# Another hand-written order of the steps, their lags and their PSUM banks, in a two-block kernel on one core

## The reference, cut to what matters

```
x = x + attn(layernorm(x))      # gated delta rule, 16 heads of 64
x = x + ffn(layernorm(x))       # softmax attention, then a mixture of 8 experts, 2 chosen
```

## Time and profile before

| | us |
|---|---|
| median of 3 runs | 5533.0 (5532.9 to 5550.23) |
| the profiled execution | 5533.59 |
| its span | 5531.7 |
| PE / DVE / ACT / POOL busy | 4792.2 / 4623.1 / 3445.0 / 2085.5 |

### The profile page before, as it was taken

The page is one execution under the profiler, slowest core; times in us unless marked ns, Lnnn a source line. Parts: engine busy times, 40 slices in busy tenths (PEclk is TensorE's granted clock), DMA queues, the critical chain, the costliest instruction groups (busy, mean ns, idle before and its releaser), DMA issues.

```text
span 5531.7 us, 111231 instructions
## 1 busy us (share of the span) xinstructions
PE 4792.2 (87%) x40448; PEld 3609.5 (65%) x40448; DVE 4623.1 (84%) x11457; ACT 3445.0 (62%) x6166; POOL 2085.5 (38%) x1485
## 2 busy tenths in 40 slices
PE   4688889988889898889898899888899888899986
PEld 2466667666667666667666677666677666677665
DVE  6888898888888888988888988888988888988852
ACT  3456666656666656766666666566666666666653
POOL 3443333443343442343443344433434433334420
PEclk7778898888888888988888888878988888888878
DMA  1001111011111011111111111111111011111011
GB/s 59 10 11 34 43 43 34 28 32 37 43 43 34 24 32 41 43 33 32 33 33 42 43 33 32 32 34 43 43 34 32 32 34 43 43 34 32 31 34 56
DMA packets 214453, 197.13 MB, mean 36 GB/s; under 512 B 13848, under 2 KB 176416, under 8 KB 209696
## 3 DMA queue, kind: packets, MB, share of 16 engines
q1 hardware_dynamic: 213920, 190.01, 11.1%
...
## 4 chain that ended last, share of the span: by engine, by line
DVE 52%; PE 38%; issue 8%; ACT 1%; SPq 0%; DMA 0%; POOL 0%; DVEq 0%; POOLq 0%; ACTq 0%
PE bank L984 36%; DVE acc L1390 10%; DVE tmpb L1556 6%; DVE NP L1526 6%; DVE Gam L1559 5%; DVE mx L1653 3%; DVE Gam L1512 3%; DVE moe L1738 2%; PE bank L988 2%; DVE QK L1671 1%; DVE QK L1479 1%; DVE Gam L1563 1%; DVE rot L1475 1%; DVE ms L1603 1%; DVE Kt L1543 1%
## 5 line engine op out<-in xcount | busy, mean ns | idle before, releaser
L1390 DVE SCALAR_TENSOR_TENSOR acc<-bank,conv_w,acc 128x255 f32<-128x255 f32 (+2 forms) x2304 | 925.1, 470 | 27.3 <-ACT acc L791 26.4
L717 POOL TENSOR_TENSOR sq<-acc 128x256 f32<-128x256 f32 x256 | 191.2, 747 | 1734.5 <-ACT acc L797 1722.3
L984 PE MATMUL bank<-QK 64*128 64x256 f32 (+1 forms) x4096 | 603.3, 352 | 211.8 <-DVE mx L1653 97.7
L984 PE MATMUL bank<-W,h 128*128 128x128 f32 x4096 | 579.7, 302 | 190.1 <-issue 103.3
L984 PEld LDWEIGHTS bank<-W,h 128*128 128x128 f32 x4096 | 551.7, 215 | 237.1 <-issue 129.6
L984 PE MATMUL bank<-mT,W 128*128 128x256 f32 x2048 | 626.4, 447 | 60.3 <-issue 39.7
L984 PEld LDWEIGHTS bank<-QK 64*128 64x128 f32 (+1 forms) x4096 | 288.6, 142 | 523.7 <-issue 346.0
L966 ACT ACTIVATE h<-bank,b 128x256 f32<-128x256 f32 x1024 | 416.7, 479 | 288.6 <-PE bank L984 286.7
L984 PEld LDWEIGHTS bank<-mT,W 128*128 128x128 f32 x2048 | 420.9, 220 | 219.2 <-issue 155.3
L729 POOL TENSOR_TENSOR rot<-rot,sin 128x512 f32<-128x512 f32 x256 | 337.3, 1317 | 450.8 <-DVE rot L1475 450.8
L1559 DVE TENSOR_TENSOR Gam<-Gam,tmpb 128x31 f32<-128x31 f32 (+15 forms) x992 | 448.1, 452 | 34.1
...
## 6 DMA issues: line engine op xcount, KB each, us to landing
W<-in_W SPq DMA_DIRECT2D x512, 256.0 KB, 3.2
...
```

Source lines behind the costliest of these rows:

```text
L984: return mm(out_, lhsT, rhs, start=first, stop=last)
L1390: v.scalar_tensor_tensor(acc[:, n % 2, m, j:T], ps[:, m, 0:T - j], conv_w[:, kind, c, PAD - j:KT - j], acc[:, n % 2, m, j:T], ALU.mult, AL ...
```

## The change

Only the two tables differ; no step is added or taken away (13 entries for SP, 43 for POOL, 120 for ACT, 173 for PE and 167 for DVE in both), and the code of the steps is the same. The place where a turn begins is another, so some lags are one higher; the number of turns is the same. Of the 170 uses of PSUM 148 have another bank. The core of the diff, by engine; each excerpt begins and ends in the middle of the list:

```diff
 "pe":
-        ... qk:4@0 sums:2@0 st:15@2 qk:6@0 qk:5@0 pv:3@2 join1:0@1 sums:3@0
-        join1:1@1 ctx:0@2 join2:0@1 join2:1@1 ctx:1@2 top:0@1 ctxT:0@2 top:1@1 cross:0@1 fWo:0@2 cross:1@1 low:0@1
-        sums:4@0 low:1@1 qk:7@0 S:0@1 o:1@1 KS:0@1 KS:1@1 QS:0@1 o:0@1 top:2@1 sums:5@0 top:3@1 cross:2@1 mT:0@2
-        cross:3@1 router:0@2 low:2@1 QS:1@1 low:3@1 up:1@2 up:0@2 o:2@1 o:3@1 alpha:1@0
+        ... qk:2@0 pv:2@2 st:13@2 qk:3@0 sums:0@0
+        st:14@2 st:15@2 join1:0@1 sums:1@0 join1:1@1 join2:0@1 pv:3@2 join2:1@1 qk:4@0 top:0@1 ctx:0@2 ctx:1@2 top:1@1
+        ctxT:0@2 sums:2@0 fWo:0@2 cross:0@1 cross:1@1 low:0@1 qk:5@0 low:1@1 o:0@1 mT:0@2 S:0@1 o:1@1 KS:0@1 KS:1@1
+        QS:0@1 up:0@2 qk:6@0 sums:3@0 sums:4@0 top:2@1 QS:1@1 up:1@2 qk:7@0 router:0@2
+        (the next turn begins)
+        sums:5@1 cross:2@2 top:3@2 low:2@2 GT:0@1 cross:3@2 alpha:0@1 up:2@3 low:3@2 o:2@2 o:3@2 sums:6@1 g:0@2 ...
 "dve":
-        ... solve:24@1 solve:25@1 qk:3@0 solve:26@1 solve:27@1 solve:28@1
-        solve:29@1 solve:30@1 close:0@1 rope:1@0 swap:3@0 qk:4@0 ctx:0@2 qk:5@0 ctx:1@2 rope:2@0 cross:0@1 rope:3@0
-        x2:0@2 cross:1@1 swap:4@0 swap:5@0 rope:4@0 fstat:2@2 qk:6@0 KS:0@1 fshift:2@2 KS:1@1 qk:7@0 o:0@1 QS:0@1
-        swap:6@0 o:1@1 cross:2@1 cross:3@1 router:0@2 ms:0@1 rope:5@0 swap:7@0 QS:1@1 choice:0@2 o:2@1
-        (the next turn begins) stat:0@0 o:3@2 alpha:0@1 ...
+        ... solve:24@1 solve:25@1 swap:0@0 solve:26@1 solve:27@1 solve:28@1 solve:29@1 solve:30@1 close:0@1 qk:2@0 rope:0@0
+        swap:1@0 expert:7@3 qk:3@0 swap:2@0 rope:1@0 ctx:0@2 ctx:1@2 qk:4@0 x2:0@2 cross:0@1 fstat:2@2 cross:1@1
+        fshift:2@2 rope:2@0 swap:3@0 swap:4@0 qk:5@0 rope:3@0 o:0@1 KS:0@1 o:1@1 KS:1@1 swap:5@0 QS:0@1
+        (the next turn begins)
+        ms:0@2 rope:4@1 stat:0@0 qk:6@1 router:0@3 QS:1@2 cross:2@2 qk:7@1 cross:3@2 rope:5@1 GT:0@1 swap:6@1 choice:0@3
+        o:2@2 o:3@2 shift:0@0 alpha:0@1 ...
 "act": (the chained stretch)
-        ... join1:0@1 tap:5@0 join1:1@1 upper:0@1 join2:0@1 join2:1@1 top:0@1 silu:4@0 ctxT:0@2 top:1@1 silu:5@0
-        square:4@0 low:0@1 low:1@1 tap:6@0 square:5@0 S:0@1 tap:7@0 silu:6@0 ln3:0@2 top:2@1 top:3@1 mT:0@2 ...
+        ... join1:0@1 upper:0@1 tap:3@0 join1:1@1 join2:0@1 silu:2@0 context:1@2 square:2@0
+        join2:1@1 top:0@1 tap:4@0 ctxT:0@2 silu:3@0 top:1@1 silu:4@0 low:0@1 ln3:0@2 square:3@0 low:1@1 tap:5@0 S:0@1
+        silu:5@0 mT:0@2 square:4@0 osq:0@1 gelu:0@2 tap:6@0 square:5@0 gelu:1@2 top:2@1 ...
 "pool":
-        ... Dv:0@1 R1:0@1 dots:6@0 R1:1@1 sin:5@0 Dv:1@1 cos:6@0 QSadd:0@1 root:0@1 QSadd:1@1
+        ... Dv:0@1 sin:4@0 cos:5@0 R1:0@1 Dv:1@1 QSadd:0@2 R1:1@2 dots:5@1 rstd:0@0 QSadd:1@2 ...
...
 BANK (of 170 uses, a few of the chained stretch)
-    top:0=3 top:1=5 top:2=6 top:3=0 ... KS:0=2 KS:1=6 QS:0=1 QS:1=0 S:0=6
+    top:0=0 top:1=0 top:2=0 top:3=1 ... KS:0=7 KS:1=2 QS:0=3 QS:1=3 S:0=7
```

More of the change, by code:

```diff
@@ L59 @@
+        Dv:0@1 sin:4@0 cos:5@0 R1:0@1 Dv:1@1""",
     "act": """
[L60 to L68, removed]
@@ new lines @@
+        tap:7@1 ex:0@3 top:3@2 silu:6@1 low:2@2 square:6@1 low:3@2 silu:7@1 gelu:2@3 g:0@2 g:1@2 g:2@2 square:7@1
+        osq:1@2 gelu:3@3 osilu:0@2 g:3@2 sums:0@1 yT:0@2 osilu:1@2 yT:1@2 vtap:0@1 yT:2@2 gelu:4@3 yT:3@2 vtap:1@1
+        vsilu:0@1 vsilu:1@1 xln:0@0 vcopy:0@1 ln1:0@2 diag:0@1 ln2:0@2 vtap:2@1 hT:0@2 xT:0@0 gelu:5@3 gelu:6@3 gelu:7@3
+        vcopy:1@1 diag:1@1 vtap:3@1 rep:0@2 diag:2@1 gate:0@0 rep:1@2 diag:3@1 alphas:0@0 rep:2@2 vsilu:2@1 tap:0@0
+        rep:3@2 vcopy:2@1 rep:4@2 vsilu:3@1 silu:0@0 rep:5@2 gelu:8@3 gelu:9@3 gelu:10@3 vcopy:3@1 rep:6@2 gelu:11@3
@@ new lines @@
+        rep:7@2 gelu:12@3 tap:1@0 square:0@0 gelu:13@3 gelu:14@3 gelu:15@3 silu:1@0 att:0@2 att:1@2 att:2@2 att:3@2
+        att:4@2 att:5@2 att:6@2 att:7@2 context:0@2 att:8@2 att:9@2 square:1@0 att:10@2 att:11@2 att:12@2 tap:2@0
+        att:13@2 att:14@2 att:15@2 join1:0@1 upper:0@1 tap:3@0 join1:1@1 join2:0@1 silu:2@0 context:1@2 square:2@0
+        join2:1@1 top:0@1 tap:4@0 ctxT:0@2 silu:3@0 top:1@1 silu:4@0 low:0@1 ln3:0@2 square:3@0 low:1@1 tap:5@0 S:0@1
+        silu:5@0 mT:0@2 square:4@0 osq:0@1 gelu:0@2 tap:6@0 square:5@0 gelu:1@2 top:2@1""",
@@ L99 @@
 }
 BANK = """
[L101 to L110, removed]
@@ L111 @@
-    st:10=5 st:11=6 st:12=7 st:13=3 st:14=5 st:15=3 sums:0=4 top:0=3 top:1=5 top:2=6 top:3=0 v:0=7 v:1=4 v:2=6 v:3=1
-    vT:0=3 vT:1=2 vT:2=0 vT:3=4 wT:0=2 xT:0=0 y:0=4 y:1=6 y:2=0 y:3=6 y:4=4 y:5=4 y:6=5 y:7=5 yT:0=1 yT:1=1 yT:2=5
-    yT:3=4"""
+    GT:0=1 KS:0=7 KS:1=2 QS:0=3 QS:1=3 S:0=7 Wo:0=5 alpha:0=0 alpha:1=0 alpha:2=5 alpha:3=2 alpha:4=2 alpha:5=3
+    alpha:6=6 alpha:7=4 alpha:8=3 alpha:9=1 alpha:10=7 alpha:11=0 alpha:12=2 alpha:13=5 alpha:14=4 alpha:15=0
+    alphaT:0=7 b2:0=0 cross:0=5 cross:1=3 cross:2=2 cross:3=7 ctx:0=7 ctx:1=2 ctxT:0=6 fWo:0=1 fqk:0=3 fv:0=2 g:0=1
```

68 lines of the change are left out of this document (38 added, 30 removed).

## The result

The changed kernel takes 6087.2 us (median of 4 runs, 6078.9 to 6091.4) against 5535.4 for the kernel before on the same chip: ratio 1.0989, interval 1.0965 to 1.1013. It is slower, as forecast, but by 552 us where 116 were forecast, and outside the range.

The account below looks back on a forecast made before the run. PE at its lower clock bounds the chained stretch, DVE the rest: 63.0 + 108.6 = 171.6, less 0.6, is 171.0 us against 167.0; 29 x 4.0 = 116 on 5533.6 gives 5650 us, range 5420 to 5715.

Parts of the forecast that it names:

- the lower level: PE's clock at 1.2 GHz in place of 2.4, forecast to last until the block of KS and QS.
- rivals 1 and 3: In the stretch from close to o:3: 1, clock returns early, 5453 us, chance 0.27; 3, never falls, 5186 us, 0.09.
- Rival 4: The order is only rotated and the turn stays at 167 us; chance 0.03.
- the point on which this rested: Full-size steps standing alone between small products leave PE's clock down; a block of 128-row products some 10 us long restores it.
- The chained stretch: Part of a turn from close to o:3, where DVE waits for PE's products: forecast 44.0 + 17.9 + 1.1 = 63.0 us.
- Outside: 109.96 - 6.8 + 5.4 = 108.6.: Rest of the turn: DVE's busy time, less its work moved away, plus its idle time, in us.
- rival 2: DVE's 5.4 us of idle time outside falls to 2: 167.6 us a turn, 5551 us; chance 0.11.
- DVE is the bound there: Outside the stretch from close to o:3, DVE sets the pace: busy for 109.96 of 115.4 us.
- one turn of 168.3 us: The old turn used for the sum: 52.9 + 109.96 + 5.4 us, while the mean turn was 167.0.
- Moving `tap:5`, costed at nothing: ACT's tap:5 behind low:1 makes DVE wait some 5 us, but it would wait for KS:0 anyway, inside the 63.0.
- The banks: New PSUM banks for PE's products: costed at nothing, between -1 and +2 us a turn.

Follow-up runs that it names:

- before_qk6_top: Kernel before with PE's qk:6 moved behind join2:1 and top:0 placed between it and ctx:1: 5579.5 us, ratio 1.0077.
- after_norm_short: Changed kernel with POOL's two multiplications of norm:1 done for one head of 16: 5982.7 us, 1.0824 to the kernel before.
- its control: Kernel before with the same cut of POOL's norm:1 to one head of 16: 5560.5 us, ratio 1.0064.
- after_wt_moe: Changed kernel with wT:0 and moe:0 one or two places later in DVE's list: 6098.6 us, 1.1046 to the kernel before.
- the fill in both kernels: 25 extra full-size PE products a turn ahead of small steps: kernel before 5378.8 us, 161.2 a turn; changed kernel 5889.0 us, 175.4 a turn.
- after_fill: Changed kernel with 25 extra full-size PE products a turn ahead of the 32x32 and 64x64 steps: 5889.0 us, 1.0618 to the kernel before.

## Why the prediction was wrong

*Direction and the work counted in were right.* PE's work from `join1:0` to `QS:0` was forecast as 44.0 us and is 44.0; DVE's work in the stretch as 41.3 and is 41.8; the clock is 0.50 there, and low until `QS:0`, as forecast. So the lower level lasts through the stretch up to `QS:0`, and rivals 1 and 3 are out (`o:0` takes 3.67 us). Rival 4 is out by the same rows. `before_qk6_top` agrees with the point on which this rested: a `qk` with a 64x64 step at its back didn't bring the clock back early.

*The chained stretch: 66.5 us for 63.0.* The step took it that PE begins `join1:0` when `close` ends; it begins 2.2 us late, behind `st:14` and `st:15`, which wait for ACT, and PE waits another 1.0 for ACT ahead of `qk:7`. What follows `QS:0` is 1.3 us over the forecast in all. Together 3.5 of the missing 12.6 us of this turn.

*The step that failed: "Outside: 109.96 - 6.8 + 5.4 = 108.6."* It is 117.7. Two assumptions are in it.

First, that DVE's instructions "are the same" and so take the same time. DVE's busy time outside is 107.6 us, not 103.2: 4.5 us. Some 3.6 of them are `norms:0` beside POOL's `norm:1`, shown by `after_norm_short` and its control. A moved step brings its neighbours on other engines with it, and I counted only its own engine's.

Second, that 5.4 us of idle time stay 5.4; they are 10.1. I had weighed only that they could shrink (rival 2). Behind it is "DVE is the bound there", read from 109.96 busy of 115.4. The new order took DVE work out of this part, and PE's chain then held it up: `after_wt_moe` took away 1.9 us of DVE's waits and gained nothing, and the chain that ended last runs for 62% over PE, where it ran for 38% before. I read it so: moving work of the busier engine out of a part shortens that part only until the next engine's chain is as long. The forecast also said nothing of the clock outside the stretch, where PE is at the lower level for 12 us more; no run separates what that costs.

*A slip in the sum.* It added up one turn of 168.3 us and set the result, 171.0, against the mean of 167.0. Against its own turn it foresaw 2.7 us more, not 4.0.

*Where the 16.8 us a turn are, by runs:* 3 to 3.6 are POOL's norm (`after_norm_short`). The 13 us more at the lower clock in the first 55 us are worth 3 to 6, an estimate with two sources. With the fill in both kernels 14.2 remain, which leaves 2.6. In the kernel before, turns with a clock of 0.78, 0.72 and 0.66 there last 164, 167 and 170 us, 6 us for 13 us at the lower level. The rest, some 7 to 11 us, comes with the order itself, the clock outside the stretch included: more work of both engines in a stretch that is a chain (55.9 us against 45.0 with the clock up; 3.9 of these 10.9 are `after_fill`'s clock of 0.93, by which 7.8 us ran at half speed), while the part outside didn't get shorter by what left it. Which single wait outside sets its 117 us stays open: those of DVE that I took away moved elsewhere. Moving `tap:5`, costed at nothing, gave some 1 us.

*The banks* I costed at nothing. One of them, `ctx:1` in bank 2, was tried only together with the order: with `top:0` moved, another bank is worth some 129 us (6144.8 to 6016.2), or 106 by the ratios.
